# Value products gathered into waves of two or three key tiles, side work put between them, and a wait inside the first weight casts

## The reference, cut to what matters

```python
q = split_heads(layernorm(x) @ Wq + bq)            # 8 heads of 4
k, v = split_heads(ctx @ Wk + bk), split_heads(ctx @ Wv + bv)
attn = softmax(q @ k.T / sqrt(32))                 # 2048 x 1601 for each head
x = x + tanh(g_x) * ((attn @ v) @ Wo + bo)
xf = layernorm(x)
G, idx = top_k(softmax(xf @ router_w + router_b).T, 512)   # per expert
h1 = relu(xf[idx] @ w1 + b1);  eo = h1 @ w2 + b2
x = x + tanh(g_f) * scatter_add(idx, eo * G)
```

## Time and profile before

| | us |
|---|---|
| median of three runs | 592.31 (591.82 to 592.48) |
| profiled execution | 591.86 |
| its span | 590.1 |
| outside the span | 1.76 |
| attention units 0 to 15, 48.33 to 340.48 | 292.15 |
| after the attention | 250 |

### The profile page before, as it was taken

One profiled execution on the slowest core, in us unless ns is written; L12 is line 12 of the kernel. 1 busy time (PEld: TensorE's weight loads), 2 busy tenths in 40 slices (PEclk: granted clock), 3 DMA queues, 4 the chain that ended last, 5 costly groups with the idle time before them and its releaser, 6 DMA issues.

```text
span 590.1 us, 12821 instructions
## 1 busy us (share of the span) xinstructions
PE 549.7 (93%) x5043; PEld 318.8 (54%) x5043; DVE 446.4 (76%) x811; ACT 391.0 (66%) x762; POOL 214.4 (36%) x205
## 2 busy tenths in 40 slices
PE   7798899999999999999998988899999999999994
PEld 4433333334343333433333344479889898898973
DVE  3889879996999969899896268656767868676541
ACT  2587778987789878898887830054665656555651
POOL 3058075001925018200167010240644626446234
PEclk9999999999999999999999999999999999999998
DMA  8600000001000000100000105012735656355133
GB/s 280 244 2 1 1 1 3 2 1 38 2 37 2 2 37 1 38 1 2 37 37 2 38 18 163 18 55 81 167 110 108 153 134 144 107 109 160 19 37 36
DMA packets 23808, 35.80 MB, mean 61 GB/s; under 512 B 3460, under 2 KB 16197, under 8 KB 23621
## 3 DMA queue, kind: packets, MB, share of 16 engines
q1 hardware_dynamic: 17604, 26.59, 13.9%
q0 software_dynamic: 6144, 8.39, 8.1%
HBM read 26.59 MB, written 8.39 MB: 59 GB/s over the span
## 4 chain that ended last, share of the span: by engine, by line
PE 72%; DVE 17%; issue 4%; ACT 3%; POOL 1%; DMA 1%; POOLq 0%; DVEq 0%; ACTq 0%; SPq 0%
PE ps L1728 15%; PE ps L1735 15%; PE ps L1497 14%; DVE mquart L1025 9%; PE ps L1463 7%; PE ps L1484 7%; PE ps L1393 2%; PE ps L1354 2%; ACT probs L752 2%; PE ps L1369 1%; PE ps L1706 1%; PE ps L1681 1%; DVE mparts L1041 1%; PE ps L1506 1%; ACT osb L651 1%
## 5 line engine op out<-in xcount | busy, mean ns | idle before, releaser
L1025 DVE TENSOR_REDUCE mquart<-ps 128x2 f32<-128x802 f32 x256 | 240.6, 986 | 28.4 <-PE ps L1463 25.9
L752 ACT ACTIVATE probs<-ps 128x512 f32<-128x512 f32 (+1 forms) x416 | 223.6, 596 | 27.0 <-PE ps L1484 22.6
L1497 PE MATMUL ps<-probs,vp 128*32 128x256 f32 (+1 forms) x1664 | 133.5, 393 | 4.2 <-ACT osb L651 4.1
L1463 PE MATMUL ps<-kpad,qrows 64*128 64x401 bf16 x512 | 89.6, 337 | 5.9 <-DVE mquart L1025 5.0
L1484 PE MATMUL ps<-qfull,kpad 64*128 64x256 bf16 (+1 forms) x832 | 86.8, 273 | 1.1 <-ACT x L773 0.9
L1322 DVE TENSOR_TENSOR h1l<-hf,h1h 128x512 fp32r<-128x512 f32 x64 | 44.3, 692 | 55.8 <-ACT hf L877 45.9
L876 ACT ACTIVATE h1h<-ps,b1T 128x512 fp32r<-128x512 f32 x64 | 43.9, 687 | 54.3 <-PE ps L1728 52.5
L1735 PE MATMUL ps<-w2h,h1h 128*128 128x256 f32 x256 | 73.8, 288 | 2.2 <-DVE h1l L1322 1.5
L1735 PE MATMUL ps<-w2l,h1h 128*128 128x256 f32 x256 | 72.4, 283 | 0.0
L1735 PE MATMUL ps<-w2h,h1l 128*128 128x256 f32 x256 | 72.3, 282 | 0.0
L621 POOL DMA_INDIRECT out<-eo,idx_put x32 | 55.4, 1732 | 26.1 <-ACT eo L886 16.9
(11 more groups left out here) (200 smaller groups left out, 732.5 us busy)
## 6 DMA issues: line engine op xcount, KB each, us to landing
w1raw<-in_L_ffn_w SPq DMA_DIRECT2D x16, 512.0 KB, 4.7
w2raw<-in_L_ffn_w SPq DMA_DIRECT2D x16, 512.0 KB
xs<-in_x SPq DMA_DIRECT2D x4, 512.0 KB, 7.8
ctx_sb<-in_ctx SPq DMA_DIRECT2D x3, 512.0 KB, 6.0
out<-xs SPq DMA_DIRECT2D x3, 512.0 KB, 4.3
x_rows<-x SPq DMA_DIRECT2D x3, 512.0 KB, 2.6
b2b<-in_L_ffn_b SPq DMA_DIRECT2D x1, 1024.0 KB, 11.6
out<-xs SPq DMA_DIRECT2D x2, 256.0 KB, 2.0
```

The costliest lines, as they stand in the source:

```text
L752: nc.scalar.activation(out_p, ps[0:w, next_bank(), :], ACT.Exp, scale=float(SCALE)).then_inc(s_ex, 1)
L1025: nc.vector.tensor_reduce(mquart[:, u % 2, t, a, :, kq], ps[:, b:b + 2, 0:MAXW], AX.X, ALU.max).then_inc(s_mr, 1)
L1463: last = mm(ps[:, bank + b, 0:MAXW], qrows[band(b), g, q:q + P], kpad[band(b), g, a, lo:lo + MAXW], start=True, stop=True)
L1497: last = mm(ps[32 * hh:32 * hh + 32, PV, 0:UW], vp[0:w, kt, g, hh, :], probs[0:w, step % PROBS, hh, :], start=(kt == 0), stop=(kt == NKT - 1))
```

## The change

The value waves of a unit, but the last unit, are gathered: instead of one wave at every key tile there are six groups, at key tiles 1 (two waves), 4 (three), 6, 8, 10 and 12 (two each). The last unit keeps one wave a key tile. The unit's output is taken one key tile later. The side work is moved, most of it to key tiles without waves; `PLACE` goes from 10 to 11; the next chunk's transposes go to key tiles 0 and 3 from the second chunk on. The statistics of both layernorms are issued two tiles at a time, and `ln2_aggr` is issued at key tile 5 instead of 8. In `first_weights` GpSimd waits before its third pair until the maxima of all 16 units are done.

```diff
-        PLACE = 10
-        O_THIS, O_LAST, BACK_AT, WO_AT = (2, 4), (0, 4), (0, 7), (0, 12)
-        XN_AT, Q_AT = ((0, 9), (0, 11)), ((1, 3), (1, 6))
-        X2_AT, ROUTER_AT = ((2, 6), (2, 7)), ((2, 9), (2, 12))
+        PLACE = 11
+        O_THIS, O_LAST, BACK_AT, WO_AT = (2, 5), (0, 5), (0, 7), (0, 9)
+        XN_FIRST, XN_LATER, Q_AT = ((0, 7), (0, 9)), ((0, 0), (0, 3)), ((1, 3), (1, 7))
+        X2_AT, ROUTER_AT = ((2, 7), (2, 9)), ((2, 10), (3, 0))
...
-        LN1_AT = {(u, NKT - CT + t): (c, t) for c, u in ((2, 1), (3, PER_CHUNK + 1)) for t in range(CT)}
-        LN2_AT = ((1, 4), (1, 5), (1, 6), (1, 7))
+        LN1_AT = {(u, kt): (c, ts) for c, u in ((2, 1), (3, PER_CHUNK + 1)) for kt, ts in ((7, (0, 1)), (8, (2, 3)))}
+        LN1_DONE = {(1, 9): 2, (PER_CHUNK + 1, 9): 3}
+        LN2_AT = {3: (0, 1), 4: (2, 3)}
+        def xn_at(c):
+            return XN_FIRST if c == 0 else XN_LATER
+        PV_GROUPS = {1: (-2, -1), 4: (0, 1, 2), 6: (3, 4), 8: (5, 6), 10: (7, 8), 12: (9, 10)}
+        def values_at(u, kt):
+            ks = PV_GROUPS.get(kt, ()) if u < UNITS - 1 else (kt - 2,)
+            return [(u, k) if k >= 0 else (u - 1, NKT + k) for k in ks if u > 0 or k >= 0]
+        def take_at(u):
+            return 2 if u < UNITS - 1 else 1
...
                 for pair in range(PAIRS):
                     a, f = 2 * P * pair, 2 * pair
+                    if pair == PAIRS // 2:
+                        pool.wait_ge(s_mp, UNITS)
...
-                    if kt == 1 and u > 0:
+                    if kt == take_at(u) and u > 0:
                         take_o(u - 1)
...
-                    if c > 0 and (r, kt) in LN2_AT:
-                        ln2_stats(c - 1, LN2_AT.index((r, kt)))
-                    if c > 0 and (r, kt - 1) == LN2_AT[-1]:
+                    if c > 0 and r == 1:
+                        for t in LN2_AT.get(kt, ()):
+                            ln2_stats(c - 1, t)
+                    if c > 0 and (r, kt) == (1, 5):
                         ln2_aggr(c - 1)
...
-                    if kt > 1:
-                        pv(u, kt - 2)
-                    elif u > 0:
-                        pv(u - 1, NKT - 2 + kt)
+                    for step in values_at(u, kt):
+                        pv(*step)
```

More of the change, by code:

```diff
@@ L822, in _ @@
                             scale_wo(c - 1, odd, next_bank())
-                    if c + 1 < NC and (r, kt) in XN_AT:
-                        take_xn(c + 1, XN_AT.index((r, kt)), next_bank())
+                    if c + 1 < NC and (r, kt) in xn_at(c):
+                        take_xn(c + 1, xn_at(c).index((r, kt)), next_bank())
                     if c + 1 < NC and (r, kt) in Q_AT:
@@ L1121, in _ @@
                         normalise(c - 1, 1, 0, next_bank())
-                    if c > 0 and (r, kt) in LN2_AT:
-                        ln2_stats(c - 1, LN2_AT.index((r, kt)))
-                    if c > 0 and (r, kt - 1) == LN2_AT[-1]:
+                    if c > 0 and r == 1:
+                        for t in LN2_AT.get(kt, ()):
+                            ln2_stats(c - 1, t)
+                    if c > 0 and (r, kt) == (1, 5):
                         ln2_aggr(c - 1)
                     if (u, kt) in LN1_AT:
-                        ln1_stats(*LN1_AT[u, kt])
-                    if kt == 0 and (u - 1, NKT - 1) in LN1_AT:
-                        ln1_aggr(LN1_AT[u - 1, NKT - 1][0])
+                        to, ts = LN1_AT[u, kt]
+                        for t in ts:
+                            ln1_stats(to, t)
+                    if (u, kt) in LN1_DONE:
+                        ln1_aggr(LN1_DONE[u, kt])
                     if (u, kt) == (UNITS - 1, 0):
@@ L1618, in _ @@
                         wo(c - 1, range(CT), (even, next_act((s_wt, 2 * c))))
-                    if c + 1 < NC and (r, kt) in XN_AT:
-                        k = XN_AT.index((r, kt))
+                    if c + 1 < NC and (r, kt) in xn_at(c):
+                        k = xn_at(c).index((r, kt))
                         transpose_xn(c + 1, k, next_act((s_Tt, KD * (c + 1) + k + 1)))
```

## The result

The changed kernel takes 618.66 us (617.03 to 621.98) against 592.37 for the kernel before: ratio 1.0453, 95% interval 1.0402 to 1.0503. The forecast was 587.0, range 573 to 595. The change makes the kernel 26 us slower. The second rival (608) named the direction and the groups, though not the right ring.

The account below looks back on a forecast made before the run. TensorE was taken to bound the units with side work, VectorE's floor most others. Terms -11.6 + 0.4 - 0.2 + 1.4 - 4.3 + 9.0 = -5.3 us on 591.86 gave 586.6, median 587.0, range 573 to 595.

Parts of the forecast that it names:

- second rival: Attention units: every group starves VectorE's two bank pairs, 0.25 us for each of 90 groups, 22.5 us, total 608; chance 0.08.
- What bounds the kernel: Attention units: TensorE is busiest in the eight with side work; VectorE's 16 reductions of 0.98 us are unit 3's floor.
- The price of a wave: TensorE: a following wave costs 0.43 us, a lone one 0.57 plus some 0.2; gathering saves 2.4 us a unit.
- The rings: Score hand-over to VectorE and ScalarE: groups of two just fit, the three starves VectorE 0.2 us in seven units, +1.4.
- side units: Units 1, 4, 5, 6, 8, 9, 10 and 12, carrying side work: from 155.15 to 143.6 us together, -11.6.
- Side work: Jobs moved to key tiles without a wave: each charged an entry of 0.2 us on TensorE, ends 0 and 0.41.
- Unit 13: VectorE's operation on the maxima waits for GpSimd's train, from about 4.5 to 14.0 us after the aggregation: +9.0 us.
- first rival: Unit 13: VectorE gets in after one GpSimd operation, 0.6 us on average in place of 9.0, total 578.6; chance 0.33.
- Unit 14 and the wait: First weights: with GpSimd's wait the 3.67 us hold in unit 14 goes, unit at 16.95 us, -4.3; work behind it free.

Follow-up runs that it names:

- e15: Kernel e2 with each maximum tile cut to one bank (half of the heads), score ring kept at three banks: 576.00 us.
- e2: Changed kernel with one value wave at every key tile again and without GpSimd's wait, so only side work, PLACE and statistics moved: 588.46 us, ratio 0.993.
- e16: Kernel e2 with one-bank maximum tiles (half of the heads) and a score ring of five banks in units 1 to 13: 571.60 us.
- e14: Changed kernel (gathered waves) with one-bank maximum tiles (half of the heads) and a score ring of five banks in units 1 to 13: 559.99 us.
- e10: Kernel e2 with a single pair of waves gathered in each of units 0 to 14 (key tile 5's wave goes to 6): 592.72 us.
- e1: Kernel before with only the value waves gathered (output taken at key tile 2), side work and GpSimd queue as before: 617.54 us, ratio 1.043.
- e8: Kernel before with a small f32 VectorE tensor_tensor on two SBUF inputs behind each maximum reduction of units 13 and 14: 592.91 us.
- e4: Changed kernel with each group issued right behind the scores, ahead of the key tile's second maximum tile: 626.98 us, ratio 1.0596.
- e7: Changed kernel with each group issued between the two scores of its key tile: 621.03 us, ratio 1.0495.
- e3: Kernel before with only GpSimd's wait before the third pair of first weights added: 589.77 us, ratio 0.9941.
- e5: Changed kernel with every maximum reduction over half the columns of its two banks: 611.31 us.
- e12: Kernel before with VectorE probes behind the maximum reductions of units 13 and 14, of the held operation's types (f32 and bf16 inputs, bf16 output): 593.08 us.

## Why the prediction was wrong, step by step

- **What bounds the kernel.** Right as far as it went: TensorE where there is side work, VectorE at its floor elsewhere. Even there VectorE's floor has the next one close under it: with the reductions halved and one wave a key tile (e15) unit 3 still takes 15.20, for 15.70 in e2. And engines that lie within 1 us of each other are bound by the loop between them as well, which busy time does not show.
- **The price of a wave.** Right. Three waves take 1.43 us (280.17 to 281.60 below), 0.57 and twice 0.43, and with five banks most of the saving is there: unit 4 goes from 18.63 in e16 to 16.73 in e14, 1.9 of the 2.4 us that I took.

```profile
280.17 1.02 PEld L1518 LDWEIGHTS ps<-probs,vp 128*32 128x32 f32 x24 [0.27 <-ACT probs L770]
281.60 0.12 PEld L1505 LDWEIGHTS ps<-qfull,kpad 64*128 64x128 bf16 x4 [0.41 <-issue]
```

- **The rings.** This is the step that failed. I wrote that "twos just fit" and took 1.4 us, and gave the side units their gain of 11.6. For TensorE I had 1.2 + 0.6 = 1.8 us; measured are 1.49, and 0.43 for the way from the scores' issue to the exponential's start, which I had left out: 1.92. For ScalarE I had three exponentials at 0.6, 1.8; but in a row they take 0.49 each (four take 2.06), and the group starts only after the second scores have waited for a bank, so there is never more in hand than these three: 1.41. The difference, 0.51 us, is what ScalarE stands still at the pair that starts at 285.91. The measured price, with its saving taken off, is 0.28 us for a single pair (e10, a mean of unlike units); for gathering as a whole 25.3 us over 90 groups, also 0.28 (e1). It isn't confined to the units that VectorE bounds: in the profiled executions the eight side units, which were to give 11.6 us, take 15.9 more, and units 2, 3, 7 and 11 together 10.5 more. The second rival's 0.25 a group stood beside the saving and not behind it, so it was too small as well, and it named the wrong ring: halving the reductions left units 3, 7 and 11 where they were.
- **Side work.** I charged 0.2 us for each job at a key tile without a wave. No run shows that term: e2 has a wave at every key tile, and there the new places come out even with the old ones outside unit 14; what a single job costs between bf16 matmuls was not measured.
- **Unit 13.** Wrong by its whole 9.0 us. The operation fell where I had put it, 4.3 us after the aggregation and in the middle of the norm, and took 0.20 us; what the unit gained in length, 16.79 to 18.12, it has in e1 too (18.04).

```profile
323.73 0.37 DVE L983 BATCH_NORM_AGGREGATE mv<-stats 128x2 f32<-128x6 f32 x4
...
328.06 0.20 DVE L1059 TENSOR_TENSOR mparts<-nmax,mparts 128x8 bf16<-128x8 f32 x1
```

```profile
325.75 4.83 POOL L555 TENSOR_SCALAR x<-xs,mv,rstd 128x256 f32<-128x256 f32 x4 [0.20 <-POOL rstd L493]
```

  The first of these fences is VectorE's timeline, the second GpSimd's. I took the nearest row of another kind of GpSimd operation for this one. The first rival was nearer, but not by its mechanism: the operation wasn't held at all. The Trainium skill (SBUF — State Buffer, "SBUF: two separate sides") gives the hold for one instruction, which the probes beside casts and the large tensor_tensor operations confirm to 0.05 us; it also names every GpSimd operation that reads SBUF, and the norm reads SBUF and held nothing in six cases (five probes of e8 and this operation). In e4 and e7 it did hold the same operation, but not for the whole instruction (last section).
- **Unit 14 and the wait.** The mechanism was right: the operation took 0.20 us. Alone the wait takes 3.7 us from unit 14, but part comes back behind the units, and 2.5 to 3.1 are left, not 4.3 (e3). In the changed kernel, whose groups lengthen the unit, 1.8 are left in it (21.24 to 19.40). With the side work moved and no wait the operation isn't held either (e2), if only by 0.07 us.
In unit 4 it follows pauses of TensorE of 0.60 us before the projection and 0.46 behind it (0.92 and 0.74 for its weight loads). They aren't the cause of the loss: e1 has only the one in unit 0 and loses 25.3 us all the same. What one costs is shown roughly by unit 4 of e5 (half of the reductions), which has none and takes 21.61 for 22.97. The stretch in unit 4:

```profile
145.60:149.00 3.40, 3.40 (x29) 1.25 (x21) 1.90 (x3) 1.80 (x5) 2.24 (x1) 0.50 0.03 12
```

## What to carry to other kernels

Before work on one engine is gathered, walk once around the loop to each engine that it feeds: from the last buffer handed over before the group, through the group, to the first result after it, the latency of the hand-over included. If that is longer than the work that the ring can hold, the group costs the difference each time, however much it saves on the engine itself, and a busy share of 91% didn't warn of it. The saving and the ring's depth belong together: here the same gathering was worth +26.7 us with three banks and -11.6 with five. Those are kernels with half of the maxima, where VectorE is busy only some 9 us a unit; five banks with whole maxima weren't tried, as the maximum tiles need the two banks.

## What the runs showed of the hardware that I had not expected

- GpSimd's cast and its large tensor_tensor operations hold VectorE's two-input SBUF operation to the end of the one that runs: ten probes of e8, 0.28 to 0.98 us, and one of 1.55. Its tensor_scalar (the norm, f32, four operations of 1.22 us) does not hold it for the whole instruction: five probes of e8 took 0.15 or 0.16 us beside it, one of them issued 0.12 us into the first of the four. But in e4 and e7 VectorE's operation on the maxima, issued 0.10 and 0.31 us into the third of the four, took 0.51 and 0.29 us instead of 0.20, and both times ended 0.60 us into it. Issued 0.41 us or more into one (e15, e16, and 1.10 in the changed kernel) it took 0.20. Why the probe in the first was not held was not found.
- Longer holds stay unexplained: four whole operations and the rest of one in unit 14 of the kernel before (3.67 us), the rest of one and one whole in e1 (2.07) and in e16 (1.37). Ten f32 probes and as many bf16 probes each got in at the first border, and so did the operation itself in e8 and e12. What differs was not found.
- Five score banks instead of three are worth 4.4 us with a wave at each key tile, and 42.7 us when the waves are gathered, both with half of the maxima.
